# Sync's attention loop over two batches, the residual's rows on ScalarE's queue, and ScalarE's loop begun at unit 6

## The chip, the cores and the metric

The kernel runs on one core of a Trainium2 chip. Its time is device time in microseconds (us), from one execution of the whole program. Before the change the median of 3 runs is 2274.84 us (2274.13 to 2275.26). The engines are named as the profile names them: PE is TensorE, DVE is VectorE, ACT is ScalarE, POOL is GpSimd, SP is SyncE. SP does no arithmetic: it issues DMAs, and an instruction of any engine can wait for a semaphore that another engine or a landed DMA raises. A "q" behind an engine's name (SPq) marks its sequencer.

## The reference

The input x is 64 batches of 32 rows by 512 (float32). Four layers are added to it one after the other:

```
x = x + einsum('bct,bcd->bdt', x, W0[cond])                       # per-batch 32x32 mixing
x = x + (x @ base.T + bias + lora(x, adapter[b]))                 # 512x512 and rank 16
x = x + attention(x, Wq, Wk, Wv, Wo, k_cache, v_cache, block_table, seqlens)
x = x + einsum('bct,bcd->bdt', x, W3[cond])
```

The attention has 32 query heads and 8 key heads of 128. Each batch reads 16 pages of 32 cached tokens (512 in all, picked by its row of the block table) and its own 32 tokens. Scores are masked by the batch's length, go through a softmax, and the weighted values of all heads go through the 4096x512 matrix Wo into a residual sum.

## The kernel before

The rows of x are kept in 16 tiles of 128 rows, so a tile is 4 batches. In the attention stage, one unit is one key head of one batch (4 query heads by 32 tokens make 128 rows): 8 units a batch, 32 units a group of 4 batches, 16 groups, 512 units. PE's code for a unit is: the scores of the unit after next, the transposes of this unit's probabilities (line L1139 in the trace), one or two of the 48 matmuls of the previous group's output projection (L1316), and the value products of the unit before (L1285, and L1295 for the batch's own tokens at its last head).

Keys and queries are split into a rounded high part and a rest, so that they can be multiplied at the fast rate. ACT makes the high part of the keys (`k_hi`, L731) four units ahead, DVE the rest (`k_lo`, L1000) three units ahead. ACT also does the exponentials (L745) and copies the transposed probabilities out of PE's memory (L791), the own tokens' ones (L769), and a batch's heads (L752, L754). DVE does the masked maximum (L1015) and, once a group, the residual sum (`residual`, L1038), which adds the projection to the tile's rows `x2r`. In group 0 ACT and DVE also split the first half of Wo, 16 pieces of it, in the units 8 to 23 (L776 and L1044).

SP loads what a batch needs two batches ahead, into one of two sets of buffers: its queries (`load_q`), its own keys (`load_own_k`, when DVE has split the last head of the batch that the buffers held: semaphore `s_klo`), then the 16 key pages (`load_pages`: it reads 16 page numbers from the table `btab` into registers, L377, and issues 16 DMAs of 128 KB, L379), its own values (`load_own_v`), and it stores the heads that the projection of the end stage needs (`o_st`, L457). The batch's last page must have landed before ACT can split its first head, four units before that batch begins. POOL gathers the cached values by four indirect DMAs a batch.

The loops of the engines run over groups 1 to 14. Groups 0 and 15 are straight code. On ACT and PE the loop turns between unit 31 and unit 0, on DVE between units 5 and 6 (`TURN`), on POOL between 23 and 24. SP's loop body, `group`, holds four batches, the load of the next table, and two DMAs of the residual: behind the second batch's values it loads `x2r` of the group before (L455), behind the fourth batch's heads it waits for DVE's residual (`s_x2y`) and stores `x2r` (L466). After the loop and group 15, SP waits for that store, loads the last tile's rows (L473), then the weights of layer 4 (L481) and the first stored heads (`load_o`, L484) for the end stage. In the end stage, for each of the 16 tiles, the second half of Wo (split by ACT in `split_wo(1, ...)`, L776, and by DVE, L1044) is applied to the stored heads, and layer 4 is added.

The first group's tables are in place from the start:

```
(btab0[:], bt_row[:, 0:2 * NPP]), (btab[:], bt_row[:, 2 * NPP:(2 + BT) * NPP])
```

Just before the attention loop SP issues the 4 MB load of the first half of Wo (`wo_raw`, L436) and goes straight on with the loads of batch 2.

Of the kernel before, what the change touches and what calls it, by code (L numbers as in the profile page):

```python
# [21 lines left out]
F32 = mybir.dt.float32  # L22
# [37 lines left out]
RESIDUAL = UG - 1  # L60
TURN = 6
# [19 lines left out]
def build(nc, x, cond_row, id_row, bt_row, idx_pages, seq_tok, seq_all, w0, w3, wb, bias,  # L81
# [3 lines left out]
    with ctx:  # L85
# [13 lines left out]
        oT_d = nc.dram_tensor("oT_d", (NT, D, BT, T), F32, kind="Internal").ap()  # L99
# [122 lines left out]
        btab = sb("btab", [1, BT * NPP], I32)  # L222
# [67 lines left out]
        LATE = 16 * 10  # L290
# [19 lines left out]
        def _(sp):  # L310
# [45 lines left out]
            for dst, src in ((seqt[:], seq_tok), (invf, invf_c), (rowc[:], row_c), (qn_sb[:, 0, :], qn), (qn_sb[:, 1, :], kn),  # L356
                             (btab0[:], bt_row[:, 0:2 * NPP]), (btab[:], bt_row[:, 2 * NPP:(2 + BT) * NPP]), (iota[:], iota_c), (seqi, seq_all), (idxi, idx_pages)):
# [13 lines left out]
            def load_table(g):  # L371

                sp.dma_start(btab[:], bt_row[0:1, bass.ds(g * (BT * NPP) + 2 * NPP, BT * NPP)]).then_inc(s_tabin, 16)
# [64 lines left out]
            def group(g, first, last):  # L438
                for k in range(BT):
                    b = g * BT + (k + 2)  # L440
                    if not (last and k >= 2):
                        if k == 0:
                            ge(sp, s_tabin, g * 16)
                        sp.wait_ge(s_qp, g * (2 * BT) + 2 * (k + 1))
                        load_q(b, k % 2)
                        sp.wait_ge(s_klo, g * UG + HK * (k + 1))
                        load_own_k(b, k % 2)
                        load_pages(btab[0:1, k * NPP:(k + 1) * NPP], k % 2)
                        sp.wait_ge(s_po, g * BT + (k + 1))
                        load_own_v(b, k % 2)  # L450
                    if k == 3 and not last:
                        load_table(g + 1)
                    if k == 1 and not first:
                        ge(sp, s_x2yst, g * 16 - 16)
                        sp.dma_start(x2r, x2_d[bass.ds(g - 1, 1)].rearrange("a p n -> p (a n)")).then_inc(s_x2r, 16)  # L455
                    sp.wait_ge(s_ost, g * BT + (k + 1))
                    sp.dma_start(oT_d[bass.ds(g, 1), :, k, :].rearrange("a p n -> p (a n)"), o_st).then_inc(s_ostst, 16)  # L457
                    if last and k == 2:

                        sp.wait_ge(s_klo, NU - HK)  # L460
                        sp.wait_ge(s_qp, (NU - HK) // 4)
# [975 lines left out]
```

## Time and profile before

| | us |
|---|---|
| median of 3 runs | 2274.84 |
| the profiled execution, its own time | 2276.92 |
| its span, first to last instruction | 2275.1 |
| attention stage within it, about | 732 to 2080 |
| PE busy | 2229.5 (98%) |
| DVE busy | 1757.3 (77%) |
| ACT busy | 1595.5 (70%) |

The profile is of one execution. Busy time is the union of an engine's instructions; what an engine waits for does not count. Matmuls are pipelined and their ends are modelled, so PE's 98% says that PE nearly always has work, not that it is at its peak. The granted PE clock is 0.99 to 1.00 of full speed in all stages. Over the attention stage the DMA engines are busy 81% of the time and move 258 GB/s. In the chain of waits that ended last, PE holds 92% of the span, DVE 2%, SP's sequencer 2%, DMA 1%.

### The profile page before, as it was taken

What the parts mean: (1) busy time and instruction counts of PE and PEld (TensorE: products, weight loads), DVE (VectorE), ACT (ScalarE), POOL (GpSimd) and SP (SyncE); (2) the same over time, 40 slices, a digit from 0 to 9 for tenths busy, and PEclk for the clock granted to TensorE, in tenths of its full rate; (3) what the DMA queues carried; (4) which work ended last, traced back from release to release, by engine and by line L of the source; (5) the groups of instructions that cost most, each with busy time, mean ns of one, the idle gap of its engine ahead of it and who ended that gap; (6) DMA issues with size and microseconds to landing.
All of it is one profiled execution on the core that took longest, in us unless ns stands there. A gap on an engine that the chain in (4) does not pass through costs nothing.

```text
span 2275.1 us, 57159 instructions
## 1 busy us (share of the span) xinstructions
PE 2229.5 (98%) x15424; PEld 1999.8 (88%) x15424; DVE 1757.3 (77%) x5602; ACT 1595.5 (70%) x4413; POOL 600.0 (26%) x907
## 2 busy tenths in 40 slices
PE   7999999999999899999999999999999999998999
PEld 6787888888887899999999999999999999997777
DVE  3433777777777999999899899899999999994332
ACT  4423666666666988888888888888888888884221
POOL 1003444444444222222222222222222222210000
PEclk9999999999999999999999999999999999999999
DMA  5335333333336888888788888888888888874332
GB/s 171 97 111 162 103 103 99 101 103 102 99 100 191 275 263 254 262 260 259 250 257 260 255 264 256 266 258 255 266 266 251 264 264 260 255 225 172 139 131 91
DMA packets 348137, 456.05 MB, mean 200 GB/s; under 512 B 34682, under 2 KB 281018, under 8 KB 343870
## 3 DMA queue, kind: packets, MB, share of 16 engines
q1 hardware_dynamic: 308430, 315.83, 44.6%
q0 software_dynamic: 36864, 134.23, 17.9%
q10 hardware_dynamic: 2672, 4.31, 0.5%
q14 instruction: 137, 1.12, 0.2%
q8 instruction: 34, 0.56, 0.1%
HBM read 374.54 MB, written 79.69 MB: 200 GB/s over the span
## 4 chain that ended last, share of the span: by engine, by line
PE 92%; DVE 2%; issue 2%; SPq 2%; DMA 1%; ACT 1%; ACTq 0%; DVEq 0%
PE oP L1285 18%; PE S L1252 16%; PE S L1209 12%; PE oP L1209 11%; PE bank L1139 9%; PE S L1303 8%; PE bank L1316 7%; PE oP L1139 3%; PE oP L1167 2%; PE oP L1295 2%; SPq L379 1%; PE oP L1159 1%; DVE k_lo L1000 1%; PE oP L1373 1%; PE bank L1269 1%
## 5 line engine op out<-in xcount | busy, mean ns | idle before, releaser
L1285 PEld LDWEIGHTS oP<-regC,regK 128*128 128x128 f32 x4096 | 529.4, 191 | 36.3 <-issue 4.9
L1285 PE MATMUL oP<-regC,regK 128*128 128x128 f32 x4096 | 540.5, 275 | 1.2
L731 ACT CAST k_hi<-regK 128x544 fp32r<-128x544 f32 x512 | 331.5, 647 | 127.7 <-PE S L1252 118.9
L1015 DVE CUSTOM_DVE_ANT_0 regC<-S,mask 128x544 f32<-128x544 f32 x512 | 369.0, 721 | 66.7 <-issue 59.0
L745 ACT ACTIVATE regC<-regC,nmx 128x544 f32<-128x544 f32 x512 | 388.0, 758 | 2.3 <-DVE nmx L1015 2.2
L1000 DVE TENSOR_TENSOR k_lo<-regK,k_hi 128x544 fp32r<-128x544 f32 x512 | 368.6, 720 | 12.7 <-ACT k_hi L731 12.7
L549 POOL COPY idx<-idx_all 128x1 int32 (+1 forms) x260 | 70.3, 273 | 963.2 <-PE oP L1295 652.0
L570 POOL TENSOR_TENSOR regC<-regC 128x256 f32<-128x256 f32 x320 | 245.4, 788 | 279.3 <-DVE regC L975 278.3
L1139 PE MATMUL bank<-ident,regC 128*128 128x128 f32 x2048 | 307.3, 272 | 2.8 <-ACT regC L791 2.8
L791 ACT COPY regC<-bank 128x512 f32<-128x512 f32 x512 | 298.7, 583 | 5.0 <-PE bank L1139 5.0
L552 POOL DMA_INDIRECT regK<-v_cache,idx x256 | 269.8, 1054 | 115.0 <-issue 114.2
L1252 PE MATMUL S<-k_hi,q_hi 128*128 128x288 f32 (+1 forms) x1024 | 256.7, 332 | 8.8 <-DVE nmx L1015 8.4
L1027 DVE TENSOR_SCALAR regC<-regC,rinv 128x512 f32<-128x512 f32 x512 | 246.8, 482 | 0.0
L1139 PEld LDWEIGHTS bank<-ident,regC 128*128 128x128 f32 x2048 | 243.6, 141 | 3.3 <-issue 3.3
L1252 PE MATMUL S<-k_hi,q_lo 128*128 128x288 f32 (+1 forms) x1024 | 213.8, 290 | 0.0
L1252 PE MATMUL S<-k_lo,q_hi 128*128 128x288 f32 (+1 forms) x1024 | 212.8, 289 | 0.0
L975 DVE SCALAR_TENSOR_TENSOR regC<-oP,rstd,regK 128x128 f32<-128x128 f32 x640 | 172.8, 343 | 8.3
L975 DVE SCALAR_TENSOR_TENSOR regC<-S,rstd,regK 128x128 f32<-128x128 f32 x640 | 172.8, 344 | 8.2
L1252 PEld LDWEIGHTS S<-k_hi,q_hi 128*128 128x128 f32 x1024 | 155.1, 191 | 23.4 <-issue 9.5
L1209 PE MATMUL S<-w_hi,x2T_hi 128*128 128x512 f32 x384 | 158.0, 411 | 4.1 <-ACT regC L682 4.1
L1252 PEld LDWEIGHTS S<-k_hi,q_lo 128*128 128x128 f32 x1024 | 157.8, 189 | 0.0
L1252 PEld LDWEIGHTS S<-k_lo,q_hi 128*128 128x128 f32 x1024 | 157.5, 189 | 0.0
(138 smaller groups left out, 4295.9 us busy)
## 6 DMA issues: line engine op xcount, KB each, us to landing
regK<-kT_cache SPq DMA_DIRECT2D x1024, 128.0 KB
qkT_d<-regC SPq DMA_DIRECT2D x160, 256.0 KB, 2.3
regC<-qkT_d SPq DMA_DIRECT2D x64, 512.0 KB, 6.3
oT_d<-regC SPq DMA_DIRECT2D x64, 256.0 KB
regK<-oT_d SPq DMA_DIRECT2D x16, 1024.0 KB, 5.4
regC<-wqk SPq DMA_DIRECT2D x10, 1024.0 KB, 5.2
v_d<-regC SPq DMA_DIRECT2D x32, 256.0 KB, 2.3
regK<-qkT_d SPq DMA_DIRECT2D x64, 128.0 KB
```

Source lines behind the costliest of these rows:

```text
L552: nc.gpsimd.indirect_dma_start(out=v_sb[par][:, m, :], out_offset=None, in_=v_cache, in_offset=bass.IndirectOffsetOnAxis(ap=idx[k][:, m:m ...
L731: nc.scalar.copy(k_hi[u % 2].rearrange("p (s t) -> p s t", t=PSIZE), k_sb[b][:, :, h, :]).then_inc(s_khi, 1)
L745: nc.scalar.activation(p, p, ACT.Exp, bias=nmx[:, u % 4:u % 4 + 1], scale=-1.0, accum_out=rs[:, u % 4:u % 4 + 1]).then_inc(s_exp, 1)
L791: nc.scalar.copy(pT_sb[u % 2], pT).then_inc(s_evA, 1)
L975: last = nc.vector.scalar_tensor_tensor(out=dst[t % 2][:, h, :], in0=bank[t % 4][:, h * D:(h + 1) * D], scalar=rstd[:, t % 4, h:h + 1], in ...
L1000: nc.vector.tensor_tensor(lo, k_sb[b][:, :, h, :], hi.bitcast(F32), ALU.subtract).then_inc(s_klo, 1)
L1015: nc.vector.tensor_tensor_reduce(out=p_sb[u % 4], in0=scores, in1=mask[:], scale=-SCALE, scalar=3e38, op0=ALU.add, op1=ALU.min, accum_out= ...
L1027: nc.vector.tensor_scalar(p[:, 0:L], p[:, 0:L], rinv[:, j:j + 1], None, ALU.mult).then_inc(s_p, 1)
L1139: last = nc.tensor.transpose(dst[:, c * P:(c + 1) * P], src[:, c * P:(c + 1) * P], ident[:])
L1209: last = nc.tensor.matmul(bank[t % 4], a[:, c, rows], w[k][:, cols], start=(c == 0 and m == 0), stop=(c == HC - 1 and m == 2))
L1252: last = nc.tensor.matmul(scores[:, at], q[u // 4 % 2][:, head], k[u % 2][:, at], start=(i == 0), stop=(i == 2))
L1285: last = nc.tensor.matmul(oP[:, at:at + P], v_sb[b][:, m, h * D:(h + 1) * D], pT_sb[u % 2][:, m * P:(m + 1) * P], start=(h < 4 and m == 0) ...
```

## The change

SP's loop now covers a pair of batches (`pair`) and runs 31 times, for all batches from 0 on; there is no straight code of a first and a last group. The table holds two batches. It is loaded by `load_table(h + 1)` behind the second batch's pages, and the first one by `load_table(0)` just behind the 4 MB load of Wo; each iteration begins with a wait for its table (`s_tabin`). The heads' store has a layout by batch, so the end stage's `load_o` reads four pieces of 2 KB a partition where it read one of 8 KB. The residual's rows are no longer SP's: ACT stores those of group g-2 behind unit 4 and loads those of group g-1 behind unit 12, and after its last unit it stores one tile's rows, waits until they have landed, and loads the last tile's. ACT's loop turns between units 5 and 6, as DVE's does.

```
+ROWS_OUT, ROWS_IN = 4, 12
...
-        oT_d = nc.dram_tensor("oT_d", (NT, D, BT, T), F32, kind="Internal").ap()
+        oT_d = nc.dram_tensor("oT_d", (B, D, T), F32, kind="Internal").ap()
...
-                             (btab0[:], bt_row[:, 0:2 * NPP]), (btab[:], bt_row[:, 2 * NPP:(2 + BT) * NPP]), (iota[:], iota_c), ...
+                             (btab0[:], bt_row[:, 0:2 * NPP]), (iota[:], iota_c), ...
...
-            def group(g, first, last):
-                for k in range(BT):
-                    b = g * BT + (k + 2)
-                    if not (last and k >= 2):
-                        if k == 0:
-                            ge(sp, s_tabin, g * 16)
...
-                    if k == 3 and not last:
-                        load_table(g + 1)
-                    if k == 1 and not first:
-                        ge(sp, s_x2yst, g * 16 - 16)
-                        sp.dma_start(x2r, x2_d[bass.ds(g - 1, 1)]...).then_inc(s_x2r, 16)
...
-                    if k == 3 and not first:
-                        sp.wait_ge(s_x2y, g)
-                        sp.dma_start(x2_d[bass.ds(g - 1, 1)]..., x2r).then_inc(s_x2yst, 16)
...
-            sp.wait_ge(s_x2yst, 16 * NT - 16)
-            sp.dma_start(x2r, x2_d[NT - 1]).then_inc(s_x2r, 16)
+            def pair(h):
+                for k in range(2):
+                    b = h * 2 + k
+                    if k == 0:
+                        sp.wait_ge(s_tabin, h * 16 + 16)
+                    sp.wait_ge(s_qp, b * 2 + 2)
+                    load_q(b + 2, k)
+                    sp.wait_ge(s_klo, b * HK + HK)
+                    load_own_k(b + 2, k)
+                    load_pages(btab[0:1, k * NPP:(k + 1) * NPP], k)
+                    if k == 1:
+                        load_table(h + 1)
+                    sp.wait_ge(s_po, b + 1)
+                    load_own_v(b + 2, k)
+                    store_heads(b)
...
+            load_table(0)
+            with sp.Fori(0, B // 2 - 1) as h:
+                pair(h)
+            store_heads(B - 2)
...
+            def load_rows(g):
+                ge(act, s_x2yst, g * 16)
+                act.dma_start(x2r, x2_d[bass.ds(g, 1)]...).then_inc(s_x2r, 16)
+            def store_rows(g):
+                act.wait_ge(s_x2y, g + 1)
+                act.dma_start(x2_d[bass.ds(g, 1)]..., x2r).then_inc(s_x2yst, 16)
...
+                if u == ROWS_OUT and not (fixed and g < 2):
+                    store_rows(g - 2)
+                if u == ROWS_IN and not (fixed and g < 1):
+                    load_rows(g - 1)
...
+            for u in range(TURN):
+                step(1, u)
             with act.Fori(1, NT - 1) as g:
-                for u in range(UG):
+                for u in range(TURN, UG):
                     step(g, u)
-            for u in range(UG):
+                for u in range(TURN):
+                    step(g + 1, u)
+            for u in range(TURN, UG):
                 step(NT - 1, u)
+            store_rows(NT - 2)
+            load_rows(NT - 1)
             own_turned(B - 1)
```

On SP, at the start of the attention stage, before the change (L436 is Wo, L388 the queries of batch 2, L384 its own keys, L377 the read of its page numbers):

```order
L436 DMA regA<-wo 128x8192 [waits s_qst1,s_qst0]
L388 DMA regC<-qkT_d 128x1024 [waits s_qp]
L384 DMA regK<-qkT_d 128x256 [waits s_klo]
L377 TENSOR_LOAD btab
L377 ISA x32
```

and after it (the same operations are L437, L389, L385 and L378 there, and L374 is the table):

```order
L437 DMA regA<-wo 128x8192 [waits s_qst1,s_qst0]
L374 DMA btab<-bt_row 1x32
L461 UNCONDITIONAL_BRANCH
L461 ISA
L445 ISA [waits s_tabin]
L389 ISA [waits s_qp]
L389 DMA regC<-qkT_d 128x1024
```

A DMA of 128 bytes and a wait for it have come between the 4 MB load and the loads of batch 2.

On ACT, after its last units, before the change (L791 is the copy of the last unit's probabilities, L769 that of the last batch's own tokens, L752 that of its heads):

```order
L745 ACTIVATE regC,rs<-regC,nmx 128x544 [waits s_mx]
L791 COPY regC<-bank 128x512 [waits s_pv,s_ta] x2
L769 COPY regC<-bank 128x256 [waits s_po,s_tb]
L752 COPY regC<-oP 128x512 [waits s_lo,s_po]
```

and after it (L797 is the copy of the probabilities, L775 that of the own tokens', L749 that of the heads; L769 and L765 are the store and the load of the residual's rows):

```order
L742 ACTIVATE regC,rs<-regC,nmx 128x544 [waits s_mx]
L797 COPY regC<-bank 128x512 [waits s_pv,s_ta] x2
L769 DMA x_d<-regC 128x512 [waits s_x2y]
L765 DMA regC<-x_d 128x512 [waits s_x2yst]
L775 COPY regC<-bank 128x256 [waits s_po,s_tb]
L749 COPY regC<-oP 128x512 [waits s_lo,s_po]
```

The store and the load, the second with a wait for the first one's landing, now stand ahead of the copy that PE's last value products wait for.

## Rows read from the trace of the kernel before

**Rows 1.** One group's time, busy by engine (instructions), PE clock, DMA share, GB/s
```profile
1150.90:1233.80 82.90, 82.81 (x699) 79.31 (x698) 75.73 (x246) 70.75 (x157) 20.60 (x32) 1.00 0.82 260
```

**Rows 2.** Timeline of SP, its loop's turn after group 8: start us, us
```profile
1406.34 0.48 SPq L466 DMA_DIRECT2D x_d<-regC  x1
1410.41 0.36 SPq L388 DMA_DIRECT2D regC<-qkT_d  x1
1411.04 0.35 SPq L384 DMA_DIRECT2D regK<-qkT_d  x1
```

**Rows 3.** Timeline of SP, another turn, in group 4
```profile
1072.15 0.65 SPq L466 DMA_DIRECT2D x_d<-regC  x1
1078.62 0.36 SPq L388 DMA_DIRECT2D regC<-qkT_d  x1
...
1085.06 8.66 SPq L379 DMA_DIRECT2D regK<-kT_cache  x16
```

**Rows 4.** Timeline of all engines, 1095 to 1108, idle time before in brackets
```profile
1099.90 0.65 ACT L731 CAST k_hi<-regK 128x544 fp32r<-128x544 f32 x1 [3.95 <-DMA regK<-kT_cache]
...
1101.18 0.63 PE L1139 MATMUL bank<-ident,regC 128*128 128x128 f32 x4 [2.56 <-ACT regC L791]
```

**Rows 5.** Timeline of ACT, its loop's turn in the projection stage
```profile
376.45 0.28 ACT L694 ACTIVATE regC<-oP 128x128 f32<-128x128 f32 x1 [2.03 <-PE oP L1209]
```

**Rows 6.** Timeline of DVE, first operation behind its loop's turn in the attention stage
```profile
1247.98 0.48 DVE L992 TENSOR_SCALAR mask<-iota,seqf 128x512 f32<-128x512 f32 x1
```

**Rows 7.** Timeline of SP at the start of the attention stage
```profile
735.05 0.35 SPq L436 DMA_DIRECT2D regA<-wo  x1
...
741.38 0.33 SPq L384 DMA_DIRECT2D regK<-qkT_d  x1
747.29 8.08 SPq L379 DMA_DIRECT2D regK<-kT_cache  x16
```

**Rows 8.** DMA issues, 735 to 736: KB, us from issue to landing
```profile
regA<-wo SPq DMA_DIRECT2D x1, 4096.0 KB, 15.2
regC<-qkT_d SPq DMA_DIRECT2D x1, 512.0 KB, 16.1
```

**Rows 9.** Waits of SP, 820 to 830: total us, times, longest
```profile
SPq L444 <- DMA btab<-bt_row: 1.9, 1, 1.9
```

**Rows 10.** Timeline of SP, the page loads of batch 26
```profile
1251.58 8.41 SPq L379 DMA_DIRECT2D regK<-kT_cache  x16
```

**Rows 11.** Timeline of ACT, the first key split of batch 26
```profile
1264.84 0.65 ACT L731 CAST k_hi<-regK 128x544 fp32r<-128x544 f32 x1 [0.43 <-DMA regK<-kT_cache]
```

**Rows 12.** Timeline of ACT, the first key split of batch 2
```profile
762.02 0.63 ACT L731 CAST k_hi<-regK 128x544 fp32r<-128x544 f32 x1
```

**Rows 13.** Timeline of DVE, the rest of that key
```profile
765.27 0.71 DVE L1000 TENSOR_TENSOR k_lo<-regK,k_hi 128x544 fp32r<-128x544 f32 x1
```

**Rows 14.** Timeline of ACT, the end of the attention stage
```profile
2059.69 0.37 ACT L769 COPY regC<-bank 128x256 f32<-128x256 f32 x1 [0.76 <-PE bank L1269]
...
2074.02 1.90 ACT L836 CAST o_hi<-regK 128x2048 fp32r<-128x2048 f32 x1 [10.15 <-DMA regK<-oT_d]
```

**Rows 15.** Timeline of DVE there
```profile
2058.58 0.69 DVE L1038 TENSOR_TENSOR regC<-bank,regC 128x512 f32<-128x512 f32 x1 [1.40 <-PE bank L1316]
```

**Rows 16.** Timeline of SP there
```profile
2062.75 0.43 SPq L466 DMA_DIRECT2D x_d<-regC  x1
2065.25 0.34 SPq L473 DMA_DIRECT2D regC<-x_d  x1
...
2066.15 0.91 SPq L484 DMA_DIRECT2D regK<-oT_d  x2
```

**Rows 17.** Timeline of PE there
```profile
2060.48 0.73 PE L1295 MATMUL oP<-regC,regK 32*128 32x128 f32 x16
...
2074.18 0.39 PE L1316 MATMUL bank<-wo_hi,oT_lo 128*128 128x512 f32 x1
2079.59 0.58 PE L1303 MATMUL S<-wo_hi,o_hi 128*128 128x512 f32 x1 [5.03 <-DVE wo_lo L1044]
```

More of the change, by code:

```diff
@@ L221, in build @@
         cond = sb("cond", [1, B], I32)
-        btab = sb("btab", [1, BT * NPP], I32)
+        btab = sb("btab", [1, 2 * NPP], I32)
         btab0 = sb("btab0", [1, 2 * NPP], I32)
@@ L289, in build @@
         s_l3, s_out, s_outst = sem("s_l3"), sem("s_out"), sem("s_outst")
-        LATE = 16 * 10
+        LATE = 16 * 9
         KLOAD = 16 * (NPP + 1)
@@ L369, in _, with load_table @@
                 sp.dma_start(w_raw[j], wqk[j].rearrange("p c n -> p (c n)")).then_inc(s_w, 16)
-            def load_table(g):
-                sp.dma_start(btab[:], bt_row[0:1, bass.ds(g * (BT * NPP) + 2 * NPP, BT * NPP)]).then_inc(s_tabin, 16)
+            def load_table(h):
+                sp.dma_start(btab[:], bt_row[0:1, bass.ds(h * (2 * NPP) + 2 * NPP, 2 * NPP)]).then_inc(s_tabin, 16)
             def load_pages(table, par, first=0, count=NPP):
@@ L468, in _ @@
-            group(0, True, False)
-            with sp.Fori(1, NT - 1) as g:
-                group(g, False, False)
-            group(NT - 1, False, True)
-            sp.wait_ge(s_x2yst, 16 * NT - 16)
-            sp.dma_start(x2r, x2_d[NT - 1]).then_inc(s_x2r, 16)
+            def pair(h):
[13 more added lines that the diff above has]
+                    store_heads(b)
@@ new lines, in store_heads @@
+            def store_heads(b):
+                sp.wait_ge(s_ost, b + 1)
+                sp.dma_start(oT_d[bass.ds(b, 1)].rearrange("a p n -> p (a n)"), o_st).then_inc(s_ostst, 16)
+            load_table(0)
+            with sp.Fori(0, B // 2 - 1) as h:
+                pair(h)
+            store_heads(B - 2)
+            sp.wait_ge(s_klo, NU - HK)
+            sp.wait_ge(s_qp, (NU - HK) // 4)
+            sp.wait_ge(s_po, B - 1)
+            sp.dma_start(wo3_raw, wo[1]).then_inc(s_wo_in, 16)
@@ L476, in _ @@
+            store_heads(B - 1)
             sp.wait_ge(s_klo, NU)
@@ L483, in load_o @@
             def load_o(g, i):
-                sp.dma_start(o3_raw[i], oT_d[bass.ds(g, 1)].rearrange("a p b n -> p (a b n)")).then_inc(s_o3[i], 16)
+                sp.dma_start(o3_raw[i].rearrange("p (b n) -> p b n", b=BT), oT_d[bass.ds(g * BT, BT)].rearrange("b p n -> p b n")).then_inc(s_o3[i], 16)
             def load_xy(g, i):
@@ L494, in _ @@
                 load_o(i, i)
+            sp.wait_ge(s_tabin, B // 2 * 16)
             sp.wait_ge(s_x2y, NT)
```

20 lines of the change are left out of this document (3 added, 17 removed).

## The prediction

> **What bounds the kernel now.** I read the table of busy time first, then the busy time of single groups, then the waits and timelines at the places that the change touches. In a group of the attention stage PE is busy 82.81 of 82.90 us [rows 1]. Thirteen of the fourteen groups in the loop have this length, or 0.3 us less where PE's own loop ends. So inside the loop an edit on SP or ACT gains nothing unless PE waits for it, and costs nothing while its delay stays below the slack. ACT is busy 70.75 us of those 82.90 [rows 1], which leaves 12.1 us over 32 units, 0.38 us a unit in ACT's own stream; PE uses ACT's copy of a unit later than that again.
>
> One group is longer than the others. In group 4 PE sat idle 2.56 us, waiting for ACT, and ACT had waited 3.95 us for a key page [rows 4]. The cause stands in SP's timeline. After its last DMA of an iteration, SP normally needs 3.6 us until the first of the next one (1406.34 + 0.48 = 1406.82 to 1410.41 [rows 2]), but here 5.8 us (1072.15 + 0.65 = 1072.80 to 1078.62 [rows 3]). The page loads of batch 18 then ran from 1085.06 to 1093.7 [rows 3], and the last one was there at 1099.9 [rows 4]. That delay is the loop's turn. DVE's turn in the same stage leaves no gap ahead of its next operation [rows 6]; ACT's turn in the projection stage leaves 2.03 us [rows 5]. Counted in the trace, sequencer's instructions included, one pass of these loops is 310 instructions on DVE, 399 on ACT in the projection stage, 429 on SP, 260 on ACT in the attention stage. So between 310 and 399 a loop stops being at hand when it turns. The Trainium skill, Runtime: NRT & Kernel Launch, Instruction fetch mechanics, says that a taken branch to an instruction outside a window of two pages of 256 has to fetch; the trace agrees as to the long loops, and puts the bound lower than 512.
>
> **SP's shorter loop.** A pair is about 215 instructions a pass, half of 429. It lies below 260 and 310, so I take its turn at DVE's value, near zero [rows 6]; the other bound is the old 3.6 to 5.8 us [rows 2, 3], now twice a group. With the turn at zero, SP asks for batch b+2's own keys as soon as DVE releases the buffers, and the late pages of group 4 go: minus 2.6 us in the profiled execution [rows 4]. Nothing else is late next there, since the other groups run at PE's pace. The table must be in before the new iteration begins. SP once waited 1.9 us for a table in the old code [rows 9]; that one landed about 2.6 us after its issue. In the new code four value loads, a store and the turn, about 3 us, lie between, and the wait for the released buffers behind it covers a microsecond or two more. Zero.
>
> **The residual's rows on ACT.** Two DMAs a group at about 0.35 to 0.5 us of sequencer time each (0.43 and 0.34 on SP [rows 16]), at units 4 and 12, while the engine still works on the copy issued before. Against 0.38 us a unit of idle time [rows 1] and the later use by PE, zero; if the cover were gone, at most 28 x 0.5 = 14 us, which I don't believe. Their waits are long met: DVE's residual is a unit-31 operation, 12 us ahead of unit 4, and the store lands 20 us ahead of unit 12. SP gives up the same DMAs, 0.5 us a turn, and gains no time for PE.
>
> **ACT's turn at unit 6.** About 266 instructions a pass, again below 310. ACT still has a 0.4 us copy in hand there. Zero; PE's turn stays where it was, and so does its cost.
>
> **The first table: the new wait.** Before, group 0 had its table from the start. Now SP issues `load_table(0)` right behind the 4 MB load of Wo, issued at 735.05, and waits for it before it asks for batch 2's queries. The 4 MB landed 15.2 us after issue, at 750.2, and the 512 KB load issued at 735.44 behind it took 16.1 us, to 751.5, where such a load needs some 6 us otherwise [rows 7, 8]. So what SP issues behind the 4 MB waits for it. The table goes over one engine, not sixteen, and is free when that engine's share of Wo is through, between 748 and 751; I take 749.8. From there: the queries, then the own keys 0.63 us later [rows 2] at 750.4 (before: 741.38), the first page 747.29 - 741.38 = 5.9 us behind these [rows 7] at 756.3, the last issued 8.1 us on [rows 7], at 764.4. Batch 26's last page was there 1264.84 - 1259.99 = 4.9 us after the end of its issue [rows 10, 11], batch 18's 6.2 us [rows 3, 4]; here the pages move beside POOL's gathers for batch 2 (754 to 768), but the fourth of these is held back by the stall itself, so 3.6 us, landing at 768.0. Its bounds are about 2 us (an idle queue) and 6.2.
>
> ACT split the first key of batch 2 at 762.02 [rows 12], but DVE, which sets the pace in that part of group 0, took it up only at 765.27 [rows 13]; ACT's 0.65 us before that would do at 764.6. So 768.0 - 764.6 = 3.4 us are lost, and 0.2 more because ACT's exponential of the unit before stands behind the same wait: 3.6 us. Bounds: pages at 766.2 give 1.8, at 771.6 give 7.0. Behind the waiting SP stand the loads of batches 3 and 4; batch 3's pages end near 781, with need at 785 + 3.6, so it is caught up within a pair.
>
> The Trainium skill, DMA: Bandwidth & Descriptors, Queues, rings and completion order, says that a later DMA on one engine can complete before an earlier one's other fifteen, while its semaphore lands only after that engine's earlier writes. By this the table comes at 748 to 750 rather than at 750.2 or later; by strict order of issue the term would be 4.0 to 4.5 us instead of 3.6.
>
> **The end of the stage.** After its last unit ACT now waits for DVE's residual, which ends at 2059.3 [rows 15], stores (to 2059.7), waits for the landing (store to next issue took 2.5 us on SP [rows 16]) and loads, so the copy for the own tokens moves from 2059.69 [rows 14] to about 2061.9, and PE's last value products from 2060.48 [rows 17] to about 2062.4: 1.9 us. All up to the end of the projection shifts by that, from 2074.6 [rows 17] to 2076.5. But that end isn't what PE waits for next. ACT waited 10.15 us for the first stored heads, there at 2074.02 [rows 14], and PE started the end stage 5.57 us later, at 2079.59 [rows 17], through ACT's and DVE's split of those heads, the residual and DVE's first piece of Wo. SP's load of these heads was issued at 2066.15, behind the store and load of the residual's rows [rows 16]. Without them it is issued about 3.4 us sooner against the last heads' store, which itself is 1.9 us late, less some waits: I take 0.8 sooner, and 0.2 back for pieces of 2 KB in place of 8 KB. So minus 0.6 us. Bounds: PE can't start before the projection's end plus residual and first piece, 2076.5 + 1.5, which is minus 1.6; with a landing as slow as 9.7 us against 7.9, the slowest and this one, plus 1.2.
>
> **The sum**, against the profiled execution's own time of 2276.92 (span 2275.1 and 1.8 around it): minus 2.6, plus 3.6, minus 0.6, gives 2277.3. The median of the runs shown is 2.1 below the profiled one. The profiled one without its late page would be 2274.3, next to the lowest run, 2274.13. So the runs shown have on average perhaps 0.6 us of late pages, and the new time is 2274.3 + 3.6 - 0.6, again 2277.3: 0.1% slower than the median. A run can be told from no change at about 0.2%, 4.5 us, so this is no change.
>
> **Rivals.**
> - *The table slips past the 4 MB.* If its engine is free early, or its packet isn't held, the start costs 0 to 1 us: 2273.8. For it: in the old loop a table was in before pages issued ahead of it. Against: the 512 KB load behind Wo wasn't in until 751.5 [rows 8].
> - *The first pages meet the value gathers in full* (slower side). Place: batch 2's pages, 756 to 766. Price: landing at 771.6 loses 7.0, with minus 0.6 at the end, 2280.7. It decides from a landing at 770 on, where the change passes 4.5 us. For it: batch 18's pages took 6.2 us after the last issue [rows 3, 4].
> - *ACT's loop is no longer at hand.* By the skill's page rule named above a body of 266 can reach over three pages of 256 by its place alone. The mechanism here: a turn that leaves a gap as the projection stage's, 2.03 us [rows 5], against about 1.2 us that PE's use of the copy allows, costs 0.8 to 1.5 us in each of 13 turns, some 15 us: 2292. For it: the code ahead of the loop has grown, so its place moved. Against: DVE's 310 are at hand [rows 6].
> - *SP's pair still pays 3.6 to 5.8 us a turn* [rows 2, 3], twice a group: several batches as batch 18, at 2.56 each [rows 4]; with two more, 2282.
> - *The end costs its full 1.9* because the heads' load lands later than I take it: 2279.5.
>
> **Chances.** Forecast 0.57, table slips past 0.14, gathers in full 0.11, ACT's loop 0.05, SP's turns 0.03, the end 0.06, and 0.04 for something that makes it faster, such as late pages in every plain run. Slower by over 0.2% (above 2279.4): 0.11 + 0.05 + 0.03, and 0.01 of the end, 0.20. Faster (below 2270.3): 0.03. Within: 0.77. The likeliest case's own range is 2275.6 to 2279.3; the range that takes in the slipping table and most of the gathers' case is 2273.2 to 2280.5.
>
> **What would show it.** SP's first queries of the stage at about 750 instead of 735, waiting for the table; batch 2's last page issued near 764; ACT's first split of batch 2 near 768 with a wait for a page; PE idle 2.5 to 4 us there. In the loop: no gap above 0.5 us at SP's turns, each of the 14 groups at 82.9 or 82.6, no ACT wait for pages, ACT's units 5 to 7 without a gap of more than 0.7. At the end: ACT's copy for the own tokens at 2.2 us behind PE's transposes, and the end stage begun within 1 us of its old distance from the last unit. The forecast is wrong if batch 2's pages are in by 765, if a group is longer than 83.2, or if the end stage begins over 1.5 us later.

## The result and the profile after

| | before | after |
|---|---|---|
| median, us (20 runs each) | 2273.43 (2270.14 to 2278.53) | 2276.89 (2275.38 to 2280.13) |
| ratio to before | | 1.0018, 95% interval 1.0012 to 1.0024 |
| span of the profiled execution | 2275.1 | 2277.2 |

By the ratio the changed kernel takes 4 us more. The interval leaves out 1, so it is slower, though by less than the 0.2% that was called no change. The forecast of 2277.3 holds for the sum (against the median of the first 3 runs it was a ratio of 1.0011; 1.0018 was measured). It doesn't hold for the parts, so they are read one by one.

PE's transposes at the start of groups 0 and 1, and those of the last unit, of the changed kernel (duration ns, then first and last start in us):

```profile
L1155 PE MATMUL bank<-ident,regC x1: 415/415/415, 731.5 to 731.5; 128*128 128x128 f32 x1
...
L1155 PE MATMUL bank<-ident,regC x1: 270/270/270, 824.3 to 824.3; 128*128 128x128 f32 x1
...
L1155 PE MATMUL bank<-ident,regC x1: 273/273/273, 2061.1 to 2061.1; 128*128 128x128 f32 x1
```

and of the kernel before:

```profile
L1139 PE MATMUL bank<-ident,regC x1: 415/415/415, 731.9 to 731.9; 128*128 128x128 f32 x1
...
L1139 PE MATMUL bank<-ident,regC x1: 272/272/272, 816.3 to 816.3; 128*128 128x128 f32 x1
...
L1139 PE MATMUL bank<-ident,regC x1: 273/273/273, 2057.7 to 2057.7; 128*128 128x128 f32 x1
```

Group 0 took 92.8 us instead of 84.4, so 8.4 more. Groups 1 to 15 took 1236.8 instead of 1241.4, 4.6 less. What lies behind the last unit took 216.0 (to 2277.2) instead of 217.4, 1.4 less. With a start 0.4 sooner that makes plus 2.0, the 2.1 between the spans.

**Group 0.** SP's timeline at the start of the stage, which answers to [rows 7]:

```profile
733.77 0.35 SPq L437 DMA_DIRECT2D regA<-wo  x1
734.16 0.32 SPq L374 DMA_DIRECT2D btab<-bt_row  x1
748.56 0.37 SPq L389 DMA_DIRECT2D regC<-qkT_d  x1
749.21 0.36 SPq L385 DMA_DIRECT2D regK<-qkT_d  x1
755.37 9.95 SPq L380 DMA_DIRECT2D regK<-kT_cache  x16
```

the table's wait in SP's list of waits:

```profile
SPq L445 <- DMA btab<-bt_row: 13.7, 1, 13.7
```

and the first key split of batch 2 on ACT (the row of [rows 12]), with PE behind it:

```profile
770.92 0.64 ACT L728 CAST k_hi<-regK 128x544 fp32r<-128x544 f32 x1 [9.34 <-DMA regK<-kT_cache]
771.48 0.58 ACT L797 COPY regC<-bank 128x512 f32<-128x512 f32 x1
```
```profile
772.20 1.09 PE L1155 MATMUL bank<-ident,regC 128*128 128x128 f32 x4 [8.21 <-ACT regC L797]
```

The table held SP for 13.7 us, until 748.3. It came before the last bytes of Wo, which landed at 750.9 (17.1 us after their issue), as the prediction took it. ACT then waited 9.34 us for a page, and PE 8.21 us. What PE waited for is named in its row: ACT's copy L797, the instruction that stands right behind the waiting split in ACT's queue. PE's granted clock was at its lower level (0.50) from 768.3 to 775.1, so for the first 2.9 us after that idle time; e4_table_between shows below that this cost group 0 nothing that can be seen.

**The loop.** One group, which answers to [rows 1]:

```profile
1155.50:1238.23 82.73, 82.71 (x699) 79.24 (x697) 75.67 (x246) 70.75 (x157) 20.61 (x32) 1.00 0.82 260
```

PE's idle time is 0.02 us where it was 0.09, and the group is 82.73 us instead of 82.86. A turn of SP's loop (the end of the store to the next queries), against [rows 2, 3]:

```profile
1448.97 1.83 SPq L394 DMA_DIRECT2D regK<-v_d  x4
1450.99 0.49 SPq L458 DMA_DIRECT2D oT_d<-regC  x1
1452.24 0.36 SPq L389 DMA_DIRECT2D regC<-qkT_d  x1
```

1451.48 to 1452.24 is 0.76 us where it was 3.6 to 5.8. No group has a late page; the only wait of ACT for one in the loop is 0.31 us, at batch 26.

**The end.** ACT and PE there, against [rows 14, 17]:

```profile
2062.72 0.34 ACTq L769 DMA_DIRECT2D x_d<-regC  x1
2064.78 0.35 ACTq L765 DMA_DIRECT2D regC<-x_d  x1
2065.22 0.37 ACT L775 COPY regC<-bank 128x256 f32<-128x256 f32 x1 [2.88 <-DMA x_d<-regC]
...
2075.39 1.91 ACT L852 CAST o_hi<-regK 128x2048 fp32r<-128x2048 f32 x1 [6.27 <-DMA regK<-oT_d]
```
```profile
2065.74 0.73 PE L1311 MATMUL oP<-regC,regK 32*128 32x128 f32 x16 [1.78 <-ACT regC L775]
2068.41 0.50 PE L1332 MATMUL bank<-wo_hi,oT_hi 128*128 128x512 f32 x1 [1.95 <-DVE oT_lo L1048]
...
2081.03 0.40 PE L1332 MATMUL bank<-wo_hi,oT_lo 128*128 128x512 f32 x1
2082.95 0.47 PE L1319 MATMUL S<-wo_hi,o_hi 128*128 128x512 f32 x1 [1.53 <-DVE wo_lo L1060]
```

The end stage begins 21.8 us behind the last unit's transposes, as before (2079.59 - 2057.7 = 21.9). But what sets it has changed. The stored heads were there at 2075.39, 6 us before the projection ended (2081.4); now PE waits for the chain behind its own projection. Busy time with the granted clock (the number before the last two) shows why the projection was late. The changed kernel:

```profile
2068.40:2072.40 4.00, 3.98 (x11) 3.12 (x11) 1.30 (x4) 0.72 (x3) 0.00 (x0) 0.57 0.83 253
2072.40:2076.40 4.00, 4.00 (x19) 3.23 (x18) 0.00 (x0) 1.01 (x1) 0.00 (x0) 1.00 1.02 390
```

and the kernel before, the first stretch at the projection's start, the second at the end stage's:

```profile
2063.00:2067.00 4.00, 3.84 (x17) 3.15 (x18) 1.45 (x5) 0.87 (x3) 0.00 (x0) 1.00 0.46 158
...
2081.00:2083.00 2.00, 2.00 (x7) 1.54 (x6) 2.00 (x5) 2.00 (x5) 0.00 (x0) 0.50 0.54 161
```

Here, at the end of the attention stage, each kernel has one stretch at the lower level, 1.2 of 2.4 GHz. Before, it follows the idle time of 5.03 us and falls on the end stage, whose first eight matmuls come 0.43 us apart instead of 0.23, 1.6 us in all. After, it follows idle times of 1.78 and 1.95 us and falls on the projection.

### The profile page after: what moved, and what is told of

Read it like the earlier page. It is cut to its first block, busy times and chain, and to the rows that moved or that the text cites. A ratio compares the mean times of both kernels' runs of the same rounds, so it can differ in the third digit from the quotient of the medians.

```text
span 2277.2 us, 57401 instructions
## 1 busy us (share of the span) xinstructions
PE 2231.3 (98%) x15424; PEld 2001.5 (88%) x15424; DVE 1757.2 (77%) x5602; ACT 1596.0 (70%) x4413; POOL 599.6 (26%) x907
## 4 chain that ended last, share of the span: by engine, by line
PE 94%; DMA 2%; DVE 1%; issue 1%; SPq 1%; ACT 1%; POOLq 0%; POOL 0%; ACTq 0%
PE oP L1301 19%; PE S L1268 17%; PE S L1225 12%; PE oP L1225 11%; PE bank L1155 10%; PE bank L1332 8%; PE S L1319 8%; PE oP L1155 3%; PE oP L1183 2%; PE oP L1311 2%; PE oP L1175 1%; DMA btab<-bt_row 1%; PE oP L1389 1%; PE bank L1285 1%; PE oP L1189 1%
## 5 line engine op out<-in xcount | busy, mean ns | idle before, releaser
L797 ACT COPY regC<-bank 128x512 f32<-128x512 f32 x512 | 298.8, 584 | 4.9 <-PE bank L1155 4.9
```

The lines of the kernel that those rows point to most:

```text
L797: nc.scalar.copy(pT_sb[u % 2], pT).then_inc(s_evA, 1)
```

## The experiments

The changed kernel is the base unless another is named. e1_table_first, e6_four_batches and e12_four_moved were timed in 11 or 12 executions and e8_best in 5; the others ran once, so that they are read from their one profile, and their times decide only where the difference is far above the spread of 5 to 10 us between executions. Kernels with one profile are compared inside a stage, because the attention stage began between 727.6 and 734.1 us in kernels that don't differ ahead of it.

### The table ahead of the 4 MB: e1_table_first

```
+            load_table(0)
             sp.dma_start(wo_raw, wo[0]).then_inc(s_wo_in, 16)
...
-            load_table(0)
```

> The first table's load is issued just ahead of the 4 MB load of Wo instead of just behind it; nothing else differs from the changed kernel. Theory: the whole loss at the start of the attention stage (group 0 took 92.80 us against 84.38 before) is the table's place behind the 4 MB. Then the table lands about 3 us after its issue, SP asks for batch 2's queries before 740 and for its own keys when DVE releases them, near 741.4; PE doesn't wait 8.21 us in unit 12; group 0 takes 84.2 to 84.7 us. The time is 8.4 us below the changed kernel's 2276.9, so about 2268.5, ratio to the kernel before 0.998 (0.9965 to 0.999). Rival: the value gathers beside batch 2's pages hold these up whatever the table does; then group 0 stays above 88 us and the ratio is 1.000 or more.

Measured: 2269.81 us, ratio to before 0.9979 (0.997 to 0.9988). SP and its wait:

```profile
735.97 0.26 SPq L374 DMA_DIRECT2D btab<-bt_row  x1
736.28 0.36 SPq L438 DMA_DIRECT2D regA<-wo  x1
740.32 0.36 SPq L389 DMA_DIRECT2D regC<-qkT_d  x1
```
```profile
SPq L446 <- DMA btab<-bt_row: 3.3, 1, 3.3
```

ACT's split of batch 2 has no wait, and group 0 takes 84.56 us. So the whole loss at the start was the place of one load of 128 bytes. Between the ratios, 1.0018 and 0.9979, lie 0.39%, 8.9 us (by their intervals, some 2.5 us either way); 8.2 of them stand in group 0.

### The table between two halves: e4_table_between

```
-            sp.dma_start(wo_raw, wo[0]).then_inc(s_wo_in, 16)
+            sp.dma_start(wo_raw[:, 0:H2 * T // 2], wo[0][:, 0:H2 * T // 2]).then_inc(s_wo_in, 16)
+            load_table(0)
+            sp.dma_start(wo_raw[:, H2 * T // 2:H2 * T], wo[0][:, H2 * T // 2:H2 * T]).then_inc(s_wo_in, 16)
...
-            load_table(0)
...
-                    act.wait_ge(s_wo_in, 16 * half + 16)
+                    act.wait_ge(s_wo_in, 16 * half + 32)
```

The last two lines make ACT wait for both loads of Wo before it splits the first piece.

> From the changed kernel: the 4 MB load of Wo is issued as two loads of 2 MB, and the first table's load stands between them. Theory: the table waits for the bytes that were issued ahead of it on the same queue. Behind 4 MB it landed 13.1 us after its issue; behind 2 MB it lands 6 to 8 us after it, near 742.5, so that SP asks for batch 2's own keys at 743 to 744 and its last page is issued near 757.5; group 0 takes 84.4 to 85.5 us, as most of the delay is inside DVE's slack of 3.3 us. Rival: the queue serves all that is issued at about the same time together, and the table comes when the whole 4 MB are nearly through, near 748: group 0 takes 91 us or more.

```profile
732.10 0.32 SPq L374 DMA_DIRECT2D btab<-bt_row  x1
...
740.52 0.36 SPq L389 DMA_DIRECT2D regC<-qkT_d  x1
```

From the table's issue to the queries it takes 4.35 us with nothing of Wo ahead, 8.4 with 2 MB and 14.4 with 4 MB. So the table's time grows with the bytes issued ahead of it, by 2.0 to 3.0 us a MB. Group 0 took 85.94 us, a little more than expected, and that is the first sign that the slack was less than I took:

```profile
761.03 0.64 ACT L729 CAST k_hi<-regK 128x544 fp32r<-128x544 f32 x1 [2.39 <-DMA regK<-kT_cache]
```

### The gathers behind the pages: e3_gathers_late

```
+                        if fixed and b == 2:
+                            pool.wait_ge(s_k[0], 2 * KLOAD)
```

> From the changed kernel: POOL's four gathers of batch 2's cached values wait until batch 2's key pages have landed (the table stays behind Wo). Theory: the pages of batch 2 landed 5.9 us after the last one was issued because the 2 MB of gathers shared the DMA engines with them. Without the gathers the last page lands 2 to 3.5 us after its issue near 765, ACT's first key split of batch 2 comes at 767 to 768.5 (770.92 in the changed kernel), and group 0 takes 89.0 to 90.5 us against 92.80. Rival: the pages take 5.9 us by themselves, whatever runs beside them: the split stays at 770.5 to 771.5 and group 0 at 92.8. Second rival: the later values hold up PE's value products at unit 17, and what unit 12 gains unit 17 loses, group 0 stays within 0.5 us of 92.8.

```profile
753.26 8.49 SPq L380 DMA_DIRECT2D regK<-kT_cache  x16
```
```profile
764.37 0.64 ACT L730 CAST k_hi<-regK 128x544 fp32r<-128x544 f32 x1 [5.29 <-DMA regK<-kT_cache]
```

From the first page's issue to the split 11.1 us, against 15.55 in the changed kernel: 1.5 us less for issuing, 3.0 less from there to landing. The gathers beside them cost batch 2's pages 4.4 us, and group 0 took 89.38 us. The absolute time of the split came out 3 us below the range expected, since this execution's stage began at 728.4; counted from there all is as the first theory said.

Counted from the stage's first transposes, the split stood at 30.1 us before (group 0: 84.4), at 32.6, 36.0 and 39.4 in the last two experiments and the changed kernel (85.94, 89.38, 92.80). From the second on the group is the split plus 53.3 or 53.4 us each time. So the loss begins at 84.4 - 53.35 = 31.05, and each microsecond behind it costs one. In group 0 of e4_table_between the clock stayed at its upper level, and in the other two it was at the lower one for 6.8 us around the end of the stall. The same 53.3 to 53.4 us follow the split all the same, so that the lower clock there cost under 0.1 us.

### The rows behind the last splits: e2_rows_last

```
-            store_rows(NT - 2)
-            load_rows(NT - 1)
             own_turned(B - 1)
             out_heads(NT - 1, BT - 1)
             for u in list(HEADS_AT)[:5]:
                 heads_high(NT - 1, *HEADS_AT[u][1:])
+            store_rows(NT - 2)
+            load_rows(NT - 1)
```

> From the changed kernel: at the end of the attention stage ACT stores and loads the residual's rows behind its last copies and splits, not ahead of the own tokens' copy. Theory: in the changed kernel this wait made PE idle 1.78 us ahead of its last value products, and the granted clock of 0.78 in 2070 to 2075 made the projection behind it 1.5 us longer. Both go: ACT's copy of the own tokens' probabilities follows the transposes by under 0.6 us, the projection takes 11.4 us again (12.9 in the changed kernel) and ends 3.3 us sooner. Then the first stored heads are what PE waits for again, with an idle time of 3 to 5 us ahead of the end stage, and the clock is granted at its lower level for 2 to 3 us behind it, which costs 1.3 to 1.6 us. The end stage begins 2 to 4 us sooner, and 1 to 2.5 us of it are left at the end of the span. Rival: the end of the projection sets nothing, the heads' load keeps its time, and the end stage begins where it did (within 0.5 us of the old distance from the last unit), with an idle time of 5 us.

```profile
2063.40:2067.40 4.00, 3.87 (x10) 3.14 (x11) 1.42 (x5) 0.84 (x3) 0.00 (x0) 0.57 0.92 281
2067.40:2071.40 4.00, 4.00 (x18) 3.22 (x18) 0.00 (x0) 0.95 (x1) 0.00 (x0) 1.00 1.05 393
```
```profile
2077.98 0.47 PE L1319 MATMUL S<-wo_hi,o_hi 128*128 128x512 f32 x1 [1.52 <-DVE wo_lo L1060]
```

Half right. The end stage begins 19.9 us behind the last unit's transposes (2058.1) instead of 21.8, so ACT's wait was worth 1.9 us. But the stored heads did not become what PE waits for, since the projection was long all the same: after 1.96 us of idle time the clock fell here (and in e8_best), and in the kernel before, after an idle time of the same length at the same place, it did not (nor in e10_before_again). One idle time decides nothing about the clock by itself. What else decides was not tried.

### ACT's loop at unit 0 again: e5_act_unit0

```
-            for u in range(TURN):
+            for u in range(UG):
                 step(1, u)
-            with act.Fori(1, NT - 1) as g:
-                for u in range(TURN, UG):
+            with act.Fori(2, NT - 1) as g:
+                for u in range(UG):
                     step(g, u)
-                for u in range(TURN):
-                    step(g + 1, u)
-            for u in range(TURN, UG):
+            for u in range(UG):
                 step(NT - 1, u)
```

> From the changed kernel: ACT's attention loop begins at unit 0 again (groups 2 to 14 in the loop, group 1 as straight code); all else stays. Theory: each of the 13 groups from 2 on took 82.73 to 82.78 us in the changed kernel and 82.86 before because ACT's turn no longer falls where the own tokens' copy and the exponential are due; back at unit 0 each takes 82.84 to 82.88, in sum 1.3 us more. Rival: the 0.1 us a group came from SP's shorter loop or from the residual's rows (DVE's or PE's wait for them), then the groups stay at 82.73 to 82.78.

```profile
1151.80:1234.66 82.86, 82.76 (x699) 79.25 (x698) 75.66 (x246) 70.75 (x157) 20.59 (x32) 1.00 0.81 259
```

From group 4 on each group takes 82.86 us again (groups 2 and 3: 82.83 and 82.81), with PE idle 0.10 us. So the 0.1 us a group, 1.4 us in the sum, is the gain of the moved turn.

### SP's loop over four batches: e6_four_batches

On e1_table_first:

```
-            with sp.Fori(0, B // 2 - 1) as h:
-                pair(h)
+            with sp.Fori(0, B // 4 - 1) as h2:
+                pair(h2 * 2)
+                pair(h2 * 2 + 1)
+            pair(B // 2 - 2)
```

> From the kernel with the table's load ahead of Wo (e1_table_first): SP's loop holds two pairs, four batches, about 430 instructions a pass instead of 215; the residual's rows stay on ACT and the table still holds two batches. Theory: only the length of the loop's body made SP's turn slow. Then each turn costs 2.5 to 5.5 us again between SP's last instruction of a pass and the first of the next, and in some turns the pages come late: one or more groups of the 15 are 0.3 to 3 us longer, and the median is 0.5 to 3 us above e1_table_first's 2269.8. Rival: the residual's DMAs and their waits on SP made the late page of group 4, not the turn; then with a slow turn or without one no group is longer than 82.9 us, and the time is e1_table_first's within 0.5 us.

Measured: 2276.69 us, ratio 1.0018 (1.0009 to 1.0027), where e1_table_first had 0.9979; the medians are 6.9 us apart. The turns take 2.6 to 5.1 us. SP at one of them, and the split that came late:

```profile
1735.37 0.38 SPq L459 DMA_DIRECT2D oT_d<-regC  x1
1740.63 0.35 SPq L389 DMA_DIRECT2D regC<-qkT_d  x1
```
```profile
1763.26 0.64 ACT L730 CAST k_hi<-regK 128x544 fp32r<-128x544 f32 x1 [4.13 <-DMA regK<-kT_cache]
```

Groups 1 and 12 were 2.6 and 4.5 us longer than the rest. The residual's DMAs are not on SP here, so slow turns bring late pages without them. Not every slow turn does: of 14 turns two did. The median's rise is above the 0.5 to 3 us expected.

### What makes a turn slow: e7_padded, e9_padded_65, e11_padded_moved, e12_four_moved

On e1_table_first, added to the pair with PAD = 130 or 65 (at both batches of a pass; two such waits make one instruction):

```
+                    for _ in range(PAD):
+                        sp.wait_ge(s_late, LATE)
```

and once, ahead of the loop, in e11_padded_moved (on e9) and with 56 in e12_four_moved (on e6):

```
+            for _ in range(50):
+                sp.wait_ge(s_late, LATE)
```

> From e1_table_first: SP's loop of a pair gets 130 more instructions, waits for a semaphore value that is long there, about 345 instructions a pass. Runs so far show turns of 0.2 to 0.25 us for loops of 215 to 310 instructions a pass and of 2.5 us and more for 399 and above. Theory: what decides is whether the body fits what the engine has at hand, and a body of 345 is still at hand: turn 0.2 to 0.3 us, groups at 82.76 us. Rival: the bound lies at or below about 345, the turn takes 2.5 to 5.5 us twice a group, and some pages are late: groups of up to 85 us.

> As e7_padded, with 65 waits for a long-reached value in a pass of SP's loop instead of 130: about 280 instructions a pass. The run with 130 (345 a pass) showed turns of 2.57 to 6.03 us, groups of 94 to 102 us, and a time of 2493.5; it can't say how much of that the turns did and how much the added instructions themselves. Theory: DVE's loop of 310 turned in 0.24 us, so 280 is at hand; the turn is 0.2 to 0.3 us, and with it most of the loss goes: groups of 82.8 to 85 us, whatever the waits cost by themselves. Rival: for SP the bound lies nearer to 215, turns of 2.5 us and more, groups of 85 to 92 us. Second rival: turns of 0.25 us, but each added wait costs SP so much that its pages are late all the same, groups of 86 to 92 us with short turns.

> As e9_padded_65 (280 instructions a pass, turns of 3.11 to 6.68 us on SP, where ACT's loop of 268 and DVE's of 310 turn in 0.25 us), with 50 more of the same waits once, ahead of the loop, so that the same loop body stands 50 instructions further on in SP's program. By the trace's count it ran from instruction 703 to 983, and the unpadded pair from 703 to 918 with turns of 0.23 us. Theory: not the length alone decides but whether the body reaches over one block boundary too many; the boundary that e9's body crosses at its end lies between 918 and 983, and the one a page of 256 before it between 703 and 727 (The Trainium skill, Runtime: NRT & Kernel Launch, Instruction fetch mechanics: a window of two pages of 256). Moved by 50 the body begins behind that one, and the turn is 0.2 to 0.3 us; what is then left of e9's loss (2394.8 us span) is the padding's own time. Rival: SP's bound is a length between 215 and 280 wherever the body stands; the turns stay at 3 to 7 us and the span within 30 us of e9's.

> As e6_four_batches (SP's loop over four batches, 428 instructions a pass, turns of 2.6 to 5.1 us, 2276.7 us), with 56 waits for a long-reached value once ahead of the loop. Two such waits make one instruction, so the body moves by 28, from instruction 703 to 1131 by the trace's count to 731 to 1159. Theory: what makes a turn slow is where the body's blocks lie, not its length: e9_padded_65 (703 to 983) turned in 3 to 7 us, e11_padded_moved (728 to 1008, the same body) in 0.24. Then even 428 instructions turn in 0.2 to 0.3 us here, no group has a late page, and the time falls by 5 to 8 us to 2269 to 2271.5, that of e1_table_first, whose loop holds half as many. Rival: 280 instructions could be saved by their place, 428 can't: turns of 2.5 us and more, late pages in one to three groups, and 2275 us or more.

| | instructions a pass | body, by the trace's count | turn, us | time, us |
|---|---|---|---|---|
| e1_table_first | 215 | 703 to 918 | 0.22 to 0.25 | 2269.81 (median of 12) |
| e9_padded_65 | 280 | 703 to 983 | 3.1 to 6.7 | 2396.6 (1 run) |
| e11_padded_moved | 280 | 728 to 1008 | 0.23 to 0.27 | 2285.37 (1 run) |
| e7_padded | 345 | 703 to 1048 | 2.6 to 6.0 | 2493.52 (1 run) |
| e6_four_batches | 428 | 703 to 1131 | 2.6 to 5.1 | 2276.69 (median of 12) |
| e12_four_moved | 428 | 731 to 1159 | 2.6 to 4.5 | 2272.40 (median of 11) |

A turn is the time from the branch to the next instruction, where that was not itself a wait. SP in e9_padded_65, e11_padded_moved and e12_four_moved, the last store of a pass and the first queries of the next:

```profile
1190.73 0.38 SPq L462 DMA_DIRECT2D oT_d<-regC  x1
1197.85 0.35 SPq L390 DMA_DIRECT2D regC<-qkT_d  x1
```
```profile
1127.65 0.37 SPq L462 DMA_DIRECT2D oT_d<-regC  x1
1128.78 0.36 SPq L390 DMA_DIRECT2D regC<-qkT_d  x1
```
```profile
1235.91 0.38 SPq L459 DMA_DIRECT2D oT_d<-regC  x1
1239.72 0.35 SPq L389 DMA_DIRECT2D regC<-qkT_d  x1
```

The same 280 instructions turn in 3 to 7 us at one place and in 0.24 us 25 instructions further on (I had written 50, but two waits share an instruction). That is 111 us of the kernel's time. So a bound on the length alone, as my prediction drew it between 310 and 399, is wrong: place decides for such bodies. The theories of e7_padded and e9_padded_65, which took bodies of 345 and of 280 instructions to be at hand, fell; that of e11_padded_moved held for the turns. But place did not save 428 instructions: my theory for e12_four_moved fell too. Its ratio, 0.9994 (0.9985 to 1.0004), lies between e6's and e1's, with turns as long as e6's. Its profile had one late page (group 1, 2.3 us) where e6's had two, which fits, but these are single executions; why the lateness varies so much from turn to turn stays open.

Fast turns don't bring e11_padded_moved down to e1_table_first: it is 15.6 us slower. Its groups 1 and 3 took 87.6 and 88.6 us, where ACT waited 3.8 and 4.4 us for pages with SP's turns at 0.23 us. So the added waits have a price of their own; why it falls on these two groups wasn't looked into.

The Trainium skill, Runtime: NRT & Kernel Launch, Instruction fetch mechanics, gives blocks of 256 instructions and a window of two of them. Block bounds near 715 and 971 fit e1, e9, e11, e7 and e6. They don't fit e12, whose body would cross one bound only and turned slowly all the same; there the measurement differs from the page. Blocks of 128, of which three are at hand, would fit all six (bounds near 715, 843, 971 and 1099); that is an estimate worked out from these runs, and no run was made to test it.

### The kernel before once more: e10_before_again

> The kernel before, once more, for a second profile of it. Its first profile had one late page in 16 groups (group 4, 2.7 us), with turns of SP's loop of 0.04 to 5.27 us. Theory: the turn's length varies from run to run, and with it the group in which pages are late: the groups that the turn doesn't delay take 82.86 us, one to three others 0.3 to 4 us more, not the same ones as before; at the end PE waits 4 to 6 us for the first stored heads. Rival: the late page of group 4 belongs to the kernel's layout and comes again in the same place with the same size.

Measured: 2270.61 us. Group 6 took 84.17 us and group 4 82.85; the late page moved:

```profile
1260.02 0.64 ACT L731 CAST k_hi<-regK 128x544 fp32r<-128x544 f32 x1 [2.51 <-DMA regK<-kT_cache]
```
```profile
2073.46 0.77 PE L1303 MATMUL S<-wo_hi,o_hi 128*128 128x512 f32 x1 [4.49 <-DVE wo_lo L1044]
```

So late pages belong to the old loop, not to batch 18 (no group of the changed kernel, of e1_table_first or of e8_best has one), and their size varies (2.7 and 1.3 us in two profiles). The end is as it was, with the heads as the last wait.

### A version that beats both: e8_best

e1_table_first and e2_rows_last together, and on ACT and DVE at the end:

```
-            act.wait_ge(s_wo, NT)
+            act.wait_ge(s_woh, NT)
             for h in range(H2):
+                if h == H2 // 2:
+                    act.wait_ge(s_wo, NT)
                 split_wo(1, h, wo3_raw)
...
-            residual(NT - 1)
             for h in range(H2):
+                if h == H2 // 2:
+                    residual(NT - 1)
                 split_wo(1, h, wo3_lo, wo3_raw)
```

> Three edits on the changed kernel together: the first table's load ahead of Wo (as e1_table_first); the residual's last store and load on ACT behind its last splits (as e2_rows_last); and the first eight pieces of the second half of Wo are split as soon as the first half of the last projection has been done, with DVE's residual behind them, where both engines waited for the whole projection. Theory: PE's waits at the end of the attention stage are one chain, own tokens' copy, projection, first piece of Wo. The first edit takes 8.4 us from the changed kernel, the second 1.9 (distance from the last unit's transposes to the end stage 19.90 us against 21.83), the third the idle time of 1.53 us ahead of the end stage, down to 0.3 or less. In sum 11.8 below the changed kernel's 2276.9, so 2265.1, ratio to before 0.9963 (0.995 to 0.9975). Rival: with the end stage begun 3.5 us sooner the stored heads or the tile's rows (x2) are what it waits for, and only the first edit's gain is left: ratio 0.998, and a wait of PE or DVE for a DMA shows at the first or second tile of the end stage.

Measured: 2265.31 us (2264.87 to 2266.38), ratio to before 0.9967 (0.9954 to 0.998). PE goes from the projection into the end stage without a gap:

```profile
2070.42 0.40 PE L1335 MATMUL bank<-wo_hi,oT_lo 128*128 128x512 f32 x1
2070.66 0.40 PE L1322 MATMUL S<-wo_hi,o_hi 128*128 128x512 f32 x1
```

It begins 18.3 us behind the last unit's transposes (2052.4), and 11.6 us are gone from the changed kernel's time, where 11.8 were expected. The projection still ran into the lower clock here, from 2058.1 to 2061.5, behind the idle time of 1.96 us.

## Why the prediction was right in the sum and wrong in its parts

- **The table's wait** was forecast at its place and nearly at its time: queries at 749.8, measured 748.56. Its price was mis-sized: 3.6 us forecast, 8.4 measured, beyond the upper bound of 7.0. The shift counted from the stage's start has two parts. The landing was taken as 3.6 us behind the last issue "beside POOL's gathers", with the fourth of them held back by the stall. It wasn't: POOL issued all four between 753.0 and 762.4 (the first and the last row below), among the pages, and they stretched issue and landing by 4.4 us (e3_gathers_late), so that the split came at 39.4 instead of the 36.1 forecast: 3.3 us. And the need was taken from DVE, which took up the key at 765.27: 32.7 us from the start, where the runs show 31.05. That is 1.65 us. 3.6 + 3.3 + 1.65, less the 0.2 counted apart, is 8.35. I had looked for the reader of the late key. The one that hurt stood behind the waiting instruction on the same engine, ACT's copy for PE. The prediction named only ACT's exponential as standing behind the same wait, and priced that at 0.2.
```profile
753.00 1.26 POOL L549 DMA_INDIRECT regK<-v_cache,idx  x1 [0.16 <-issue]
...
762.41 0.96 POOL L549 DMA_INDIRECT regK<-v_cache,idx  x1 [0.16 <-issue]
```

- **The rival "gathers in full"** is what happened at the start, with its landing (771.6 forecast, 770.92 measured). It had 0.11. Part of that hit is luck: the rows that the prediction gives for it, 764.4 and 6.2, add up to 770.6, and its price of 7.0 was too low by 1.4.
- **SP's turn** at 0.76 us between its DMAs and no late page: right, minus 2.8 in the profile for 2.6 forecast. What the pair loop is worth in other executions varies: with a slow turn put back the ratio to before rose from 0.9979 to 1.0018 in one placement of the code (e6) and to 0.9994 in another (e12). The argument that carried it, 215 instructions below a bound of 310, was wrong in form: e9_padded_65 shows 280 turning slowly on SP. The pair's body might have lain badly as well. The same holds for ACT's 268, which I gave 0.05.
- **ACT's turn at unit 6** was put at zero. It gives 1.4 us over the loop, shown by e5_act_unit0. PE's 0.09 us idle in [rows 1] was in sight, and I didn't ask what ended it. The 0.4 us that group 1 lost in the first profile (83.27 us; the prediction counted it among the groups of 82.9) is gone too, but in e10_before_again, the same kernel, it was 0.07, so that it isn't shown that the change brought this gain.
- **The residual's rows on ACT in the loop**: zero, as forecast; the groups with them are 82.84 us at most.
- **The end**: minus 0.6 forecast, minus 1.4 measured, by another way. ACT's wait made PE's last value products 1.8 us later, as forecast (1.9). The heads came early, also as forecast, but earlier than assumed (landing 6.9 us after issue, not 7.9), so that the projection became the bound, and that ran into the lower clock for 1.5 us more. In exchange the end stage, free of the 5 us idle time, ran at the full clock from its start. The prediction had no term for the clock in either place. Its rival for the end was also added up wrongly: 2274.3 + 3.6 + 1.9 is 2279.8, not 2279.5, and by either price all of its 0.06 belonged to "slower by over 0.2%", and not 0.01.

Start 4.8 us too low, loop 2.0, end 0.8 and the stage's beginning 0.4 too high: 1.6 us are left, where the largest error alone is three times as large, and with them 2277.3 becomes the profiled execution's own 2278.98 (the median lies lower). That the time was right says little for the working.

## What to carry to other kernels

A small load that something waits for goes ahead of the big one on its queue, not behind it. When an instruction will be late, look first at what stands behind it on its own engine, and only then at who reads its result. A loop's turn is a matter of length and of place in the program: measure the turn after every change in the code ahead of the loop.

## What the runs showed of the hardware

- The instruction that waited for a load of 128 bytes went on 4.35, 8.4 and 14.4 us after the load's issue, with 0, 2 and 4 MB issued just ahead of it on the same queue.
- The same loop of 280 instructions on SP turned in 3.1 to 6.7 us, or in 0.23 to 0.27 us when it was moved by 25 instructions, and loops of 268 on ACT and 310 on DVE turn in 0.22 to 0.25 us.
- After 1.96 us of idle time PE was granted 1.2 GHz in one kernel and 2.4 GHz in another at the same place; the lower level lasted from about 3 us (e2_rows_last) to 7 (e1_table_first, 2060.7 to 2067.6, where the end stage began 1.0 us later behind the last unit than in the changed kernel).
- In group 0 of the attention stage a stretch of 6.8 us at the lower level cost under 0.1 us of the group's time, since the work behind the late page took 53.3 to 53.4 us with it or without.
